# Four input buffers for the LayerNorm statistics and another order of the attention-value matmuls, in a transformer layer on eight cores

## The reference, cut to what matters

```python
x = x + attn(layernorm(x), Wq, Wk, Wv, Wo)      # x: (16, 2048, 1024), 16 heads of 64
x = x + ffn(layernorm(x), ...)                  # 1024 -> 4096 -> 4096 -> 4096 -> 1024

def _layernorm(x, axis=-1, eps=1e-5):
    m = jnp.mean(x, axis=axis, keepdims=True)
    v = jnp.var(x, axis=axis, keepdims=True)
    return (x - m) / jnp.sqrt(v + eps)

scores = jnp.einsum('bhnd,bhmd->bhnm', Q, K) / sqrt(d_k)
scores = jnp.where(causal, scores, -jnp.inf)
out = jnp.einsum('bhnm,bhmd->bhnd', jax.nn.softmax(scores, axis=-1), V)
```

## Time and profile before

| | us |
|---|---|
| runs of the kernel before | 8295.72 and 8762.97, median 8529.35 |
| the profiled execution | 7880.67 |
| its span on the slowest core (7) | 7879.1 |
| spans of the eight cores | 7855.2 to 7879.1 |
| TensorE busy on core 7 | 6473.8 (82%) |
| ScalarE, VectorE busy | 1243.8 (16%), 1194.5 (15%) |
| share of PE in the chain that ended last | 75% |
| share of VectorE, DMA, ScalarE in it | 8%, 7%, 6% |

### The profile page before, as it was taken

How to read it: one execution, slowest core, us unless ns; L and a number is a source line. 1 busy time by engine, 2 the same in 40 slices (tenths; PEclk the granted TensorE clock), 3 DMA queues, 4 the chain that set the end, 5 groups by cost and what they waited for, 6 DMA issues and landing times.

```text
span 7879.1 us, 73502 instructions; the slowest of 8 cores (7855.2 to 7879.1 us)
## 1 busy us (share of the span) xinstructions
PE 6473.8 (82%) x29248; PEld 2697.5 (34%) x29248; DVE 1194.5 (15%) x2035; ACT 1243.8 (16%) x1680; POOL 316.4 (4%) x603
## 2 busy tenths in 40 slices
PE   3666653666653899999689999959999995999999
PEld 0222210222211344444244444424444442444444
DVE  3244422244431200000120000021000002100000
ACT  0344420244430110000011000001000000100000
POOL 0000000000000100000010000001000000100000
PEclk7888876777876999999899999989999998999999
DMA  3100023100013444444444444434444453444444
GB/s 89 26 6 6 6 52 97 48 6 6 6 26 99 78 78 78 75 75 76 109 79 79 75 75 77 88 100 76 78 78 77 76 102 84 78 79 76 75 76 107
DMA packets 152111, 527.13 MB, mean 67 GB/s; under 512 B 17888, under 2 KB 17888, under 8 KB 114144
## 3 DMA queue, kind: packets, MB, share of 16 engines
q0 software_dynamic: 86256, 386.01, 28.2%
q1 hardware_dynamic: 65520, 136.41, 5.5%
HBM read 874.78 MB, written 33.55 MB: 115 GB/s over the span
## 4 chain that ended last, share of the span: by engine, by line
PE 75%; DVE 8%; DMA 7%; ACT 6%; issue 3%; SPq 1%; DVEq 0%; ACTq 0%; POOLq 0%
PE psA L834 22%; PE psB L834 22%; PE psA L771 3%; DMA xre<-xT 3%; PE psA L904 3%; PE psC L771 3%; PE psB L904 3%; PE psD L771 3%; PE psB L771 3%; DMA x1l<-x1s 2%; DVE scr L528 2%; PE psA L354 2%; DMA xt<-xT 2%; ACT p L491 1%; PE psC L364 1%
## 5 line engine op out<-in xcount | busy, mean ns | idle before, releaser
L834 PE MATMUL psA<-hA,hwb 128*128 128x512 bf16 x4096 | 894.5, 379 | 6.4 <-DVE hA L798 6.4
L834 PE MATMUL psA<-hB,hwb 128*128 128x512 bf16 x4096 | 894.5, 379 | 5.4 <-ACT hB L848 5.4
L834 PE MATMUL psB<-hA,hwb 128*128 128x512 bf16 x4096 | 894.5, 379 | 0.0
L834 PE MATMUL psB<-hB,hwb 128*128 128x512 bf16 x4096 | 894.5, 379 | 0.0
L921 DVE SCALAR_TENSOR_TENSOR outb<-psA,s3v,x1w 128x1024 f32<-128x1024 f32 x16 | 20.5, 1283 | 3756.1 <-PE psA L904 2853.7
L834 PEld LDWEIGHTS psA<-hA,hwb 128*128 128x128 bf16 x4096 | 400.7, 98 | 490.5 <-issue 8.3
L834 PEld LDWEIGHTS psA<-hB,hwb 128*128 128x128 bf16 x4096 | 400.8, 98 | 489.3 <-issue 7.3
L834 PEld LDWEIGHTS psB<-hA,hwb 128*128 128x128 bf16 x4096 | 400.6, 98 | 483.4
L834 PEld LDWEIGHTS psB<-hB,hwb 128*128 128x128 bf16 x4096 | 400.5, 98 | 483.6
L354 PE MATMUL psA<-qhp,khp 64*128 64x512 bf16 x640 | 243.0, 468 | 369.0 <-ACT p L493 230.7
L364 PE MATMUL psC<-p,vs 128*64 128x512 bf16 x640 | 317.1, 496 | 142.3 <-DVE p L522 100.1
(11 more groups left out here) (150 smaller groups left out, 5593.7 us busy)
## 6 DMA issues: line engine op xcount, KB each, us to landing
hwb<-h1w POOLq DMA_DIRECT2D x128, 1024.0 KB, 7.9
hwb<-h2w POOLq DMA_DIRECT2D x128, 1024.0 KB, 7.8
xt<-xT SPq DMA_DIRECT2D x128, 256.0 KB, 2.5
x1l<-x1s SPq DMA_DIRECT2D x128, 256.0 KB, 3.0
w1b<-w POOLq DMA_DIRECT2D x128, 256.0 KB, 3.6
w2b<-w POOLq DMA_DIRECT2D x128, 256.0 KB, 3.6
hwb<-w POOLq DMA_DIRECT2D x32, 1024.0 KB, 9.2
xre<-xT SPq DMA_DIRECT2D x64, 256.0 KB, 3.6
```

The costliest lines, as they stand in the source:

```text
L834: ins = t.matmul(ps_[:, nsb * 512:(nsb + 1) * 512], hwb[ot % 2][:, ic * 128:(ic + 1) * 128], src_[:, ic * 1024 + nsb * 512: ic * 1024 + ns ...
```

## The change

Three things are changed, all in the attention part.
1. The first LayerNorm pass uses all four buffers `xt[0]` to `xt[3]` in turn. A load waits for the tile four before it, and across chunks for tiles 4 to 7 of the chunk before.
2. The second pass loads into `xre[0]` and `xre[1]`, with their semaphores, and not into `xt[2]` and `xt[3]`. So it waits for `xre_free`, and the output projection after it waits for the second pass.
3. `emit_av`, called for two key tiles, becomes `emit_av_pair`: first the four value matmuls of both key tiles, then the four ones matmuls.

```diff
--- before.py
+++ after.py
@@ -241,7 +241,7 @@
         rp = [psC[:, 0:512], psC[:, 512:1024], psD[:, 0:512], psD[:, 512:1024]]
 
         st.update(bank_pj=[None] * 4, bank_pk=[None, None], wba_free=[None, None],
-                  xt_free=[None, None], stats_free=[], uv_free=None, uv2_free=None,
+                  xt_free=[None, None, None, None], stats_free=[], uv_free=None, uv2_free=None,
                   act_free=None, qk_free=None, vs_free=None, p_free=None,
                   xre_free=[None, None])
 
@@ -258,32 +258,31 @@
                 dv_base0 = sDV.n
                 def _(sy, b=b, nch=nch):
                     for ic in range(8):
-                        g_ = _aslist(st['xt_free'][ic % 2]) + [consts_ld]
-                        if ic >= 2:
-                            g_ += [(sPE, pe_base0 + ic - 1), (sDV, dv_base0 + ic - 1)]
-                        xldt.append(slot_dma(sy, sLxt[ic % 2], g_,
-                            xt[ic % 2][:, :],
+                        g_ = _aslist(st['xt_free'][ic % 4]) + [consts_ld]
+                        if ic >= 4:
+                            g_ += [(sPE, pe_base0 + ic - 3), (sDV, dv_base0 + ic - 3)]
+                        xldt.append(slot_dma(sy, sLxt[ic % 4], g_,
+                            xt[ic % 4][:, :],
                             xT[b, ic * 128:(ic + 1) * 128, nch * 512:(nch + 1) * 512]))
                 blk.sync(_)
 
                 bc_tok, rows_tok, cons1 = emit_ln_stats(
-                    lambda ic: xt[ic % 2][:, :], sq_t,
+                    lambda ic: xt[ic % 4][:, :], sq_t,
                     stp, bcp,
                     ln_state['stats_free_e' if ev else 'stats_free_o'], [],
                     xldt, ln_state['bc_free_e' if ev else 'bc_free_o'])
 
-                st['xt_free'] = [cons1[6], cons1[7]]
+                st['xt_free'] = [cons1[4], cons1[5], cons1[6], cons1[7]]
                 xldt2 = []
                 dv_base = sDV.n
                 def _(sy, b=b, nch=nch):
                     for ic in range(8):
                         g_ = list(cons1[6 + (ic % 2)])
-                        if 'xt_free2' in st:
-                            g_.append(st['xt_free2'][ic % 2])
                         if ic >= 2:
                             g_.append((sDV, dv_base + 2 * ic - 2))
-                        xldt2.append(slot_dma(sy, sLxt[2 + ic % 2], g_,
-                            xt[2 + ic % 2][:, :],
+                        g_ += _aslist(st['xre_free'][ic % 2])
+                        xldt2.append(slot_dma(sy, sLxr[ic % 2], g_,
+                            xre[ic % 2][:, :],
                             xT[b, ic * 128:(ic + 1) * 128, nch * 512:(nch + 1) * 512]))
                 blk.sync(_)
 
@@ -292,13 +291,13 @@
                     for ic in range(8):
                         wait_toks(v, [xldt2[ic]])
                         v.wait_ge(sDV.h, sDV.n)
-                        winc(sDV, v.tensor_sub(scr[:, :], xt[2 + ic % 2][:, :], bcp[:, 0:512]))
+                        winc(sDV, v.tensor_sub(scr[:, :], xre[ic % 2][:, :], bcp[:, 0:512]))
                         v.wait_ge(sDV.h, sDV.n)
                         winc(sDV, v.tensor_mul(
                             act[:, ic * N + nch * 512: ic * N + nch * 512 + 512],
                             scr[:, :], bcp[:, 512:1024]))
                 blk.vector(_)
-                st['xt_free2'] = [sDV.tok(), sDV.tok()]
+                st['xre_free'] = [sDV.tok(), sDV.tok()]
                 if ev:
                     ln_state['stats_free_e'] = [rows_tok]
                     ln_state['bc_free_e'] = [sDV.tok()]
@@ -360,20 +359,24 @@
                                 qhp[64:128, c * 512:(c + 1) * 512],
                                 start=True, stop=True, tile_position=(64, 0))
 
-            def emit_av(t, tt_, hp, ntl):
-                t.matmul(psC[0:64, 0:512],
-                         vs[:, tt_ * 1024 + (2 * hp) * 64: tt_ * 1024 + (2 * hp) * 64 + 64],
-                         p0[:, tt_ * 512:(tt_ + 1) * 512],
-                         start=(tt_ == 0), stop=(tt_ == ntl - 1), tile_position=(0, 0))
-                t.matmul(psC[64:128, 512:1024],
-                         vs[:, tt_ * 1024 + (2 * hp + 1) * 64: tt_ * 1024 + (2 * hp + 1) * 64 + 64],
-                         p1[:, tt_ * 512:(tt_ + 1) * 512],
-                         start=(tt_ == 0), stop=(tt_ == ntl - 1), tile_position=(0, 64))
-                t.matmul(psD[0:64, 0:512], ones_bf[:, 0:64], p0[:, tt_ * 512:(tt_ + 1) * 512],
-                         start=(tt_ == 0), stop=(tt_ == ntl - 1), tile_position=(0, 0))
-                return t.matmul(psD[64:128, 512:1024], ones_bf[:, 0:64],
-                                p1[:, tt_ * 512:(tt_ + 1) * 512],
-                                start=(tt_ == 0), stop=(tt_ == ntl - 1), tile_position=(0, 64))
+            def emit_av_pair(t, ta, tb, hp, ntl):
+                for tt_ in (ta, tb):
+                    t.matmul(psC[0:64, 0:512],
+                             vs[:, tt_ * 1024 + (2 * hp) * 64: tt_ * 1024 + (2 * hp) * 64 + 64],
+                             p0[:, tt_ * 512:(tt_ + 1) * 512],
+                             start=(tt_ == 0), stop=(tt_ == ntl - 1), tile_position=(0, 0))
+                    t.matmul(psC[64:128, 512:1024],
+                             vs[:, tt_ * 1024 + (2 * hp + 1) * 64: tt_ * 1024 + (2 * hp + 1) * 64 + 64],
+                             p1[:, tt_ * 512:(tt_ + 1) * 512],
+                             start=(tt_ == 0), stop=(tt_ == ntl - 1), tile_position=(0, 64))
+                ins = None
+                for tt_ in (ta, tb):
+                    t.matmul(psD[0:64, 0:512], ones_bf[:, 0:64], p0[:, tt_ * 512:(tt_ + 1) * 512],
+                             start=(tt_ == 0), stop=(tt_ == ntl - 1), tile_position=(0, 0))
+                    ins = t.matmul(psD[64:128, 512:1024], ones_bf[:, 0:64],
+                                   p1[:, tt_ * 512:(tt_ + 1) * 512],
+                                   start=(tt_ == 0), stop=(tt_ == ntl - 1), tile_position=(0, 64))
+                return ins
 
             for hp in range(8):
                 pk = [psC[:, 0:512], psC[:, 512:1024], psD[:, 0:512], psD[:, 512:1024]]
@@ -571,8 +574,7 @@
                                     if c > 0:
                                         w.append(ev_pred[c - 1])
                                 wait_toks(t, w)
-                                emit_av(t, ta, hp, ntl)
-                                ins = emit_av(t, tb, hp, ntl)
+                                ins = emit_av_pair(t, ta, tb, hp, ntl)
                                 if tb == ntl - 1:
                                     winc(sPE, ins)
                 blk.tensor(_)
```

## The result

Over 26 runs the kernel after took 8023.44 us in the median (7830.91 to 8854.12), the kernel before 8295.72 us over 25 runs (7879.22 to 8936.65). These medians say little, since an execution in which the cores of a die get a lower clock takes up to 1060 us more; the comparisons leave such executions out, and without them the ratio of after to before is 0.9943, 95% interval [0.9929, 0.9958]: about 45 us less, 0.6%. Profiled, the kernel took 7834.32 us, where the profiled execution of before took 7880.67, 46 us more.

A forecast was written before the change was run, and what follows sets the result against it. Taken as bound: load latency in LayerNorm, mutual waits of engines in attention, TensorE in dense feed-forward. 199.6 - 136 - 1.5 = 62 us of gain; 8529 - 62 = 8467 us, range 7780 to 8720.

The forecast's parts named there:

- The first pass: Attention LayerNorm's first pass with four buffers: TensorE becomes the limit, 16.4 to 17.6 us a pass, 17.0 taken.
- The gain of the first passes: Eight first passes in sum: 136 us instead of 199.6, a gain of 63.6 us.
- The prefetch: Behind a second pass's last load, four loads of the next chunk instead of two: cost 1.5 us in all.
- Second passes and attention: Second passes keep their pace, cost zero; attention stretches stay within 10 us of 855.5 and 932.3.
- The order of the matmuls: Inside emit_av, V, V, ones, ones for V, ones, V, ones: cost 0, bounds 141 us slower, about 10 faster.
- Rival 3: In emit_av the column halves stop running side by side: 0.21 us more a pair, +269 us, 8736; chance 0.04.
- Rivals 1 and 2: First pass: loads slowed by shared bandwidth, 8494 or more, chance 0.10; TensorE not holding the high clock, 8556, chance 0.05.
- Rival 4: Attention stretches change their clock: 96 us more gain beside the 62, about 8370; chance 0.04.
- The sum: Whole kernel: 199.6 - 136 - 1.5 = 62 us of gain.
- The absolute time: Whole kernel: median of the two runs shown, 8529, less 62 gives 8467 us.
- rival 5: Whole kernel: gain as worked out, but executions differ by more (7881, 8296, 8763 us); chance 0.15.
- peak-current rule: First pass: a limiter at 13/16 clock makes the fast part 16/13 as long, gain 41 us, time 8488; chance 0.03.

The follow-up runs named there:

- e5: The kernel after, unchanged, timed on one chip with e6: mean core span 7819.1 +- 2.0 us, before 7871.7 there.
- e6: The kernel after with the old emit_av order (loads alone), same chip as e5: mean core span 7823.5 +- 1.8 us, 0.993 of before.
- e4: The kernel after, unchanged, run again for stage lengths: first passes 140.3 us in sum, feed-forward LayerNorm 475.0; no total given.
- e3: The kernel before, unchanged, run again for stage lengths: first passes 192.0 us in sum, feed-forward LayerNorm 465.2; no total given.
- e7: The kernel after with three buffers instead of four in the first pass: mean core span 7830.9 +- 4.0 us, 12 over after.
- e9: Loads alone of the change (old matmul order) plus four buffers in both feed-forward LayerNorm passes: mean core span 7675.4 +- 1.5 us, 0.9717 of before.
- e11: The kernel before plus four buffers in both feed-forward LayerNorm passes: mean core span 7736.1 +- 1.1 us, 0.9796 of before.
- e1: The kernel after with the old emit_av order (loads alone): mean core span 7813.0 +- 1.8 us against 7863.6 before, ratio 0.9937.
- e2: The kernel before with only the new order of the attention-value matmuls: mean core span 7860.2 +- 2.0 us against 7863.6 before.
- e8: The kernel after with four buffers in the attention LayerNorm's second pass too: mean core span 7796.6 +- 1.5 us against 7819.1.
- e12: Against before: the change's loads, old order, four buffers in all LayerNorm passes and output projection, stores two loads later: 7529.16 and 7529.48 us, 0.954.

## Why the prediction was right and wrong

**The first pass: right.** The step said 16.4 to 17.6 us a pass and 136 in sum, bound by TensorE; measured 16.6 to 17.8 and 136.5. Load turn, slow start and pair times were each read from rows of before, and they all held.

**The gain of the first passes: mis-sized.** 63.6 us was 199.55 less 136. But 199.55 is the sum of core 7, the largest of the eight; the mean of the cores was 194.3, so the gain was 57.8. A second execution of the kernel before gave 192.0. What one core shows beyond the others in one execution is for the most part chance: core 4 ended with core 7 (7879.0 and 7879.1 us) and had 194.5.

**The prefetch: right.** 1.5 us expected, 1.1 measured (0.2 before, 1.3 after). Second passes and attention: no change expected, none measured.

**The order of the matmuls: right.** 0 expected, -3.4 +- 2.6 alone and -4.4 +- 2.7 with the loads (e5 less e6). Rival 3, 0.21 us a pair, is out; pairs are 0.21 to 0.24 us apart. Rivals 1 and 2 are out too: no first pass of after reached 20 us, and TensorE kept its high level. Rival 4 is out: attention took 1721.0 and 1720.5 us.

**The sum: wrong by a loss that it didn't hold.** 62 us were forecast and about 45 measured, 17 us short. 6 are the slowest core's surplus above, 6 are lost in the feed-forward LayerNorm, of which the prediction only said that the change doesn't touch it, and 3 in the output projections; the last 2 are less than executions scatter. It has the same two-buffer loads, so its length is load latency, and that is not a property of the stage alone. Its four stages took 465.2, 465.2 and 463.5 us in three executions with the old loads, and 463.9, 467.2, 471.3, 471.4, 475.3 and 475.6 in six with the new ones (e4's is left out for its clock; e3, e6 and e7 also had cores at a lower clock). The step to add was: what is latency-bound behind the change may be longer or shorter when the cores arrive otherwise. That the loss sits in those loads is supported by e9 and e11; what makes them later isn't settled. The spread of the cores' arrival doesn't tell the executions apart: 14 us in e1, where nothing was lost, and 20 and 22 in after and e5, but 24 and 29 in before and e2.

**The absolute time: wrong, and this is the step that failed the forecast.** 8467 was the median of two runs, 8529, less 62; the many runs since put before at 8296 and after at 8023 in the median. So 8467 lies above the later median of before: the term of the sum that was off is the 8529, by 234 us, nearly four times the gain. I took two executions, 8% above the profiled one and over 5% from each other, for the place of the distribution. That is rival 5, to which I gave 0.15: the medians differ by 272 us where the change is worth about 45. The range of 7780 to 8720 holds both medians and so says nothing about the change. The profiled time less the gain, 7819, which stands in the prediction, is 0.2 to 0.5% below eleven of the twelve executions that count (7831 to 7854; the twelfth took 7888). The forecast should have been that.

**The clock.** I set the runs above the profiled one aside as something that executions do, and gave the peak-current rule 0.03 on the strength of the 1.00 of one execution. e4 shows what it is: dense matmuls at a granted clock of 0.82 instead of 1.00 on core 0, and not on core 2 of the same die in the same stretch. The introduction to the profile ahead of the prediction says that the clock has two levels; these rows show a third. By the Trainium skill ("TensorE: Matmul & The Clock Gate", Part 1) a peak-current limit can hold a die at 13/16 of the full clock, 0.8125. Here the value agrees with the 0.81 and 0.82. That it takes the whole die doesn't agree: cores 2 and 3 kept 1.00 beside cores 0 and 1, and in the profiled execution of before all eight cores show 1.00 over the same 500 us. The price that the prediction put on it, 16/13 on the fast part or 2.7 us a pass, was right where it struck: the passes of 19.3 to 20.2 us in e8, against 17.0. It hits both kernels, so it wasn't the change.

## What to carry to other kernels

- With n buffers a load-bound loop takes (load + waits + use) / n a tile until the next engine binds. All terms are rows of one trace, and the numbers held for two, three and four buffers (194, 148, 136 us; at four TensorE binds). Count buffers against that, and look at every loop with the same pattern: four more here were worth six times the change under study.
- Take stage lengths as means over all cores before subtracting. The slowest core's surplus was mostly chance here. And don't give an absolute time from two executions that lie 5% apart: give the profiled time less the gain.
- A queue that issues loads and stores in one order prefetches nothing if a load stands behind a store that waits for a result: moving stores two loads later, with two more buffers, took the output projections from 157 us to 92 in the mean. Which of the two did how much wasn't tried.

## What the runs showed of the hardware beyond expectation

- TensorE's granted clock in a dense stretch was 0.82 on one core and 1.00 on another of the same die (e4), and 0.81 over single stretches of 10 us; executions with a lower clock take up to 1060 us more than 7880.
- The same kernel before had a mean core span of 7863.6, 7871.7, 7875.8 and 7877.3 us on four chips, each with a standard error under 2 us. The 14 us between them are over a quarter of the effect studied. Each chip was used in one session, so chip and session aren't told apart.
- A load of 256 KB took 6.18 us instead of 2.5 to 3.2 where it was issued right behind the last loads of a second pass, with three more behind it (e8). From 1045 to 1135 us, within the output projection, the eight cores moved 176 to 203 GB/s each at a DMA share of 0.71 to 0.77 (e12).
